# Keys, queries and the turn of the maxima computed by halves of the rows, each half at its own part of a stretch over two PSUM banks

## The reference

```python
h = _ln(x, g1, be1)
x = _attn(h, h, Wq1, Wk1, Wv1, Wo1, bo1) + x        # 16 heads of 64, 1024 keys for each of 1024 queries
h = _ln(x, g2, be2)
x = _attn(h, context, Wq2, Wk2, Wv2, Wo2, bo2) + x  # 64 keys
h = _ln(x, g3, be3)
y = h @ Wp + bp
a, gate = (y[..., :FF_HID], y[..., FF_HID:])
x = a * jax.nn.gelu(gate, approximate=False) @ W2 + b2 + x
```

## Time and profile before

| | us |
|---|---|
| median of 3 runs | 2045.64 (2045.41 to 2047.96) |
| the profiled execution | 2048.6 |
| its span | 2046.8 |
| TensorE busy in it | 2031.4 (99%) |
| ScalarE, VectorE, GpSimd busy | 1156.6, 1393.2, 1416.5 |

### The profile page before, as it was taken

One profiled execution on the slowest core, in us unless ns is written; L12 is line 12 of the kernel. 1 busy time (PEld: TensorE's weight loads), 2 busy tenths in 40 slices (PEclk: granted clock), 3 DMA queues, 4 the chain that ended last, 5 costly groups with the idle time before them and its releaser, 6 DMA issues.

```text
span 2046.8 us, 31824 instructions
## 1 busy us (share of the span) xinstructions
PE 2031.4 (99%) x12500; PEld 1387.6 (68%) x12500; DVE 1393.2 (68%) x2130; ACT 1156.6 (57%) x1845; POOL 1416.5 (69%) x745
## 2 busy tenths in 40 slices
PE   8999999999999999999999999999999999999999
PEld 6655655667566566665655666566558999888888
DVE  5767678665767785568678566757777888744453
ACT  4556567554556775356667544656665667533332
POOL 2599799984988998779799867979895576300000
PEclk9999999999999999999999999999999999999999
DMA  7300000001000000010000001000011420000100
GB/s 227 124 6 21 6 6 16 6 6 45 18 11 6 16 6 6 1 62 6 6 6 22 6 1 51 7 6 1 22 42 21 145 83 1 1 21 21 42 11 31
DMA packets 46565, 58.74 MB, mean 29 GB/s; under 512 B 5968, under 2 KB 40400, under 8 KB 45264
## 3 DMA queue, kind: packets, MB, share of 16 engines
q1 hardware_dynamic: 46416, 56.71, 8.9%
HBM read 38.88 MB, written 17.83 MB: 28 GB/s over the span
## 4 chain that ended last, share of the span: by engine, by line
PE 98%; DVE 1%; ACT 1%; issue 0%; DMA 0%; DVEq 0%; ACTq 0%
PE score L490 22%; PE score L473 18%; PE score L599 9%; PE score L477 6%; PE score L421 5%; PE attn_project L613 4%; PE attn_project L585 4%; PE first_score L447 4%; PE score L555 4%; PE attn_project L421 4%; PE attn_project L524 3%; PE score L433 3%; PE score L524 2%; PE attn_project L447 2%; PE first_score L514 2%; PE attn_project L433 1%
## 5 line engine op out<-in xcount | busy, mean ns | idle before, releaser
L1317 POOL TENSOR_TENSOR acc<-acc,pT 128x1024 f32<-128x1024 f32 x384 | 914.7, 2382 | 55.9 <-POOL acc L1317 1.3
L1101 ACT ACTIVATE pT<-score 128x1024 f32<-128x1024 f32 x512 | 525.7, 1027 | 102.9 <-PE score L477 60.2
L473 PE MATMUL score<-qk 64*128 64x512 f32 x3072 | 456.3, 399 | 1.5 <-ACT oT L1112 0.9
L490 PE MATMUL score<-pT,vT 128*64 128x512 f32 x2016 | 446.5, 595 | 0.0
L780 DVE TENSOR_REDUCE nmax<-first_score 128x1 f32<-128x512 f32 x512 | 347.9, 679 | 6.9 <-PE first_score L447 4.8
L780 DVE TENSOR_REDUCE nmax<-attn_project 128x1 f32<-128x512 f32 x512 | 347.1, 678 | 0.0
L473 PEld LDWEIGHTS score<-qk 64*128 64x128 f32 x3072 | 257.2, 184 | 120.7 <-ACT pT L1101 68.2
L490 PEld LDWEIGHTS score<-pT,vT 128*64 128x64 f32 x2016 | 139.2, 137 | 289.3 <-issue 251.8
L1314 POOL TENSOR_TENSOR acc<-pT 128x1024 f32<-128x1024 f32 x64 | 154.0, 2407 | 154.5 <-ACT pT L1101 154.4
L802 DVE RECIPROCAL sums<-sums 128x512 f32<-128x512 f32 (+1 forms) x65 | 214.4, 3299 | 57.5 <-ACT sums L1126 56.9
L477 PE MATMUL score<-shift,pick 64*128 64x512 f32 x1024 | 205.3, 391 | 0.0
(11 more groups left out here) (160 smaller groups left out, 3062.1 us busy)
## 6 DMA issues: line engine op xcount, KB each, us to landing
xres<-x_middle SPq DMA_DIRECT2D x10, 512.0 KB, 3.8
xres<-in_x SPq DMA_DIRECT2D x4, 1024.0 KB, 7.6
raw_qk<-in_L_xattn_Wq SPq DMA_DIRECT2D x32, 128.0 KB, 2.2
raw_qk<-in_L_xattn_Wk SPq DMA_DIRECT2D x32, 128.0 KB, 2.4
raw_v<-in_L_xattn_Wv SPq DMA_DIRECT2D x8, 512.0 KB, 4.0
keys_all<-keys SPq DMA_DIRECT2D x1, 4096.0 KB, 12.0
values_all<-values SPq DMA_DIRECT2D x1, 4096.0 KB, 12.4
out_x<-xres SPq DMA_DIRECT2D x7, 512.0 KB, 2.9
```

The source lines that it names most:

```text
L473: e.matmul(bank, qk[P % 2][r, 2 + h, keys], qk[P % 2][r, w, queries], start=(part == 0), stop=False)
L490: last = e.matmul(banks[bank][head * DH:(head + 1) * DH, :], vT[:, v_slot(D, jt), c0:c0 + DH], pT[:, jt, head, :], start=(jt == 0), stop=( ...
L1101: e.activation(pT[:, jt].rearrange("p h n -> p (h n)"), SC[R % 2][:, :], ACT.Exp).then_inc(s.exponential, 1)
L1317: e.tensor_tensor(total, total, pT[:, jt], ALU.add).then_inc(s.probs_added, 1)
```

## The change

In the 43 plain spells the work is done by halves of the rows. The maxima's transpose becomes two, each of 64 rows, one to the last 64 columns of T0 and one to the first 64 of T1, which together are one stretch of 128 columns over two banks. A projection becomes four runs of six matmuls of 64 rows by 256 columns: rows 0 to 63 and rows 64 to 127 of the operands are multiplied side by side, each half into its own half of a stretch of 512 columns, whose first 256 are the end of one bank and whose last 256 are the start of the next; then (`turn` 1) they change over, and each half adds to what the other has written. In between stands the same run of the other projection, and a new semaphore, `half_projected`, keeps the change-over behind the end of both halves' first turn. The first projection now goes to the stretch over PV and PJ, the second to the one over S1a and S1b. ScalarE and VectorE read the stretches in one instruction as before, in the same order. In the rounds that follow a plain spell, the part 1 of `first_score` is moved from round 1 to round 0. Nothing is changed in the other spells.

```diff
+        HALF = BANK // 2
+        across = {"S1": SC[1][:, HALF:HALF + BANK], "PX": PX[:, HALF:HALF + BANK],
+                  "T": FS[:, BANK - DH:BANK + DH]}
+        both = {"S1": ("S1a", "S1b"), "PX": ("PV", "PJ"), "T": ("T0", "T1")}
...
-            jobs = [("max", C + 1, "T1")] if C + 1 < NC else []
...
+            jobs = [("max", C + 1, "T1" if between else "T")] if C + 1 < NC else []
...
-                jobs += [("qk", after, 1 - c, "S1b"), ("qk", after, 3 - c, "PJ")]
+                jobs += [("qk", after, 1 - c, "S1b" if between else "PX"), ("qk", after, 3 - c, "PJ" if between else "S1")]
...
+            def project_qk_rows(P, u, pair, turn):
...
+                if turn:
+                    need.wait_ge(s.half_projected, half_of[P, u])
+                else:
+                    bank_free(*both[pair])
+                for i, (w, h) in enumerate(TERMS):
+                    for k in range(KT):
+                        for g in range(2):
+                            r, part = slice(g * DH, (g + 1) * DH), (g + turn) % 2 * HALF
+                            last = e.matmul(across[pair][:, part:part + HALF], wqk[r, P % 2, w, kind, k, :],
+                                            hT[r, h, k, c * BANK + part:c * BANK + part + HALF],
+                                            start=(i == k == turn == 0), stop=(i == 2 and k == KT - 1 and turn == 1))
+                            if i == 2 and k == KT - 1 and not turn:
+                                last.then_inc(s.half_projected, 1)
+                if turn:
+                    last.then_inc(s.qk_projected, 1)
+                    for bank in both[pair]:
+                        free[bank] = ((s.split_lo, qk_of[P, u]),)
...
+            def turn_max_rows(C):
...
+                bank_free(*both["T"])
+                for g in range(2):
+                    r = slice(g * DH, (g + 1) * DH)
+                    last = e.transpose(across["T"][:, r], maxima[r, :], ident[r, r])
+                last.then_inc(s.max_turned, 1)
+                for bank in both["T"]:
+                    free[bank] = ((s.shift_in, C + 1),)
...
-                    if job[0] == "qk":
+                    if job[0] == "qk" and job[-1] in both:
+                        project_qk_rows(*job[1:], 0)
...
+                for job in jobs:
+                    if job[0] == "qk" and job[-1] in both:
+                        project_qk_rows(*job[1:], 1)
...
-                        for head in range(2):
-                            first_score(*next_part(C + 1, jt), head)
+
+                        early = C > 0 and by_rows(C - 1)
+                        for part in {0: (0, 1), 1: ()}.get(jt, (jt,)) if early else (jt,):
+                            for head in range(2):
+                                first_score(*next_part(C + 1, part), head)
```

More of the change, by code:

```diff
@@ L21 @@
     const mask_made padded wqk_split wv_split ffn_split probs_added bias_added bias3_added scaled2 keys2_lo
-    ctx_turned ctx_product wq2_turned keys2_product values2_product ln_turned qk_projected v_projected first_scored0 first_scored1
+    ctx_turned ctx_product wq2_turned keys2_product values2_product ln_turned qk_projected half_projected v_projected first_scored0 first_scored1
     max_turned scored attended summed out1_product scored2 turned2 out2_product up_product down_product
@@ L308, in slot, with by_rows @@
             if after < B * PAIRS:
-                jobs += [("qk", after, 1 - c, "S1b"), ("qk", after, 3 - c, "PJ")]
+                jobs += [("qk", after, 1 - c, "S1b" if between else "PX"), ("qk", after, 3 - c, "PJ" if between else "S1")]
             return jobs
+        def by_rows(C):
+            return slot(C) and slot(C)[0][-1] == "T"
+        half_of = {job[1:3]: 2 * (i + 1) for i, job in enumerate(
+            job for C in range(NC) for job in slot(C) if job[0] == "qk" and job[-1] in both)}
         def last_out1(i):
@@ L412, in fold_values @@
                     free[bank] = ((semaphore, n + 1),)
+            def project_qk_rows(P, u, pair, turn):
+                kind, c = (1 if u < 2 else 0), u % 2
+                need.wait_ge(s.wqk_split, 2 * (P + 1))
+                normed((1, P // PAIRS * CHUNKS + c))
+                if turn:
[15 more added lines that the diff above has]
+                        free[bank] = ((s.split_lo, qk_of[P, u]),)
             def project_qk(P, u, bank="PJ"):
@@ L458, in turn_max @@
                 free[bank] = ((s.shift_in, C + 1),)
+            def turn_max_rows(C):
+                need.wait_ge(s.max_in, C + 1)
+                need.wait_ge(s.const, 2)
+                bank_free(*both["T"])
[5 more added lines that the diff above has]
+                    free[bank] = ((s.shift_in, C + 1),)
             def score(R, part, head):
@@ L530, in whole_array @@
                 for job in jobs:
-                    if job[0] == "qk":
+                    if job[0] == "qk" and job[-1] in both:
+                        project_qk_rows(*job[1:], 0)
+                    elif job[0] == "qk":
                         project_qk(*job[1:])
@@ L534, in whole_array @@
                         project_v(*job[1:])
+                    elif job[0] == "max" and job[-1] in both:
+                        turn_max_rows(job[1])
                     elif job[0] == "max":
@@ L773, in split_qk @@
                 hi, lo = (qk[P % 2][:, 2 * kind + w, span] for w in range(2))
-                e.scalar_tensor_tensor(lo, banks[bank], SCALE if kind == 0 else 1.0, hi.bitcast(F32),
+                e.scalar_tensor_tensor(lo, across[bank] if bank in both else banks[bank], SCALE if kind == 0 else 1.0,
+                                       hi.bitcast(F32),
                                        ALU.mult, ALU.subtract).then_inc(s.split_lo, 1)
@@ L795, in make_shift @@
                 e.tensor_tensor(shift[:, :].rearrange("p (t n) -> p t n", t=TPC),
-                                banks[bank][:, 0:PART].unsqueeze(1).to_broadcast([PART, TPC, PART]),
+                                (across[bank] if bank in both else banks[bank])[:, 0:PART].unsqueeze(1).to_broadcast(
+                                    [PART, TPC, PART]),
                                 mask[:, :].unsqueeze(2).to_broadcast([PART, TPC, PART]), ALU.mult).then_inc(s.shift_in, 1)
@@ L1081, in split_qk @@
                     need.wait_ge(s.scored, 4 * TILES * (P - 1))
-                e.activation(qk[P % 2][:, 2 * kind, c * BANK:(c + 1) * BANK], banks[bank], ACT.Copy,
+                e.activation(qk[P % 2][:, 2 * kind, c * BANK:(c + 1) * BANK],
+                             across[bank] if bank in both else banks[bank], ACT.Copy,
                              scale=SCALE if kind == 0 else 1.0).then_inc(s.split_hi, 1)
```

## The result

The changed kernel takes 2063.75 us, median of 4 runs (2062.69 to 2064.64), the kernel before 2046.80 in the same comparison (2045.41 to 2048.59): a ratio of 1.0079, 95% interval 1.0066 to 1.0091, **slower by 0.8%**. The forecast was 2063.0. The profiled execution took 2064.18 against 2048.6, +15.6 us, where the sum had said +17.4; the medians are 16.95 apart.

The account below looks back on a forecast made before the run. TensorE, busy 99% of the span, was taken to bound the kernel. 41 spells at +0.42 us (17.2) and +0.23 once gave +17.4: 2063.0 us beside the median of 2045.64, own range 2059 to 2070 (chance 0.70).

Parts of the forecast that it names:

- the sum: Whole execution: 41 plain spells at +0.42 us, 17.2, and +0.23 once, together +17.4 us.
- The passage, -0.20: From projections into round 0: array stays divided and weights load ahead, saving 0.20 us per plain spell.
- The projections, +0.09: Per plain spell, 24 pairs of 256 columns at 0.120 take 2.88 us instead of 2.79: +0.09.
- The halved transpose: Maxima's turn: two side-by-side transposes for one, first projection starts as before; bounds 0.05 us either way.
- the lower bound: Projection pairs at 0.116 us, half of 0.233: the low end of the forecast's own range, -3.9 us.
- The change-over at no cost: Between projection turns: the wait for half_projected costs nothing, as the other projection's six pairs, 0.72 us, stand between.
- The wait at round 1: Round 1's first pair waits for VectorE's lo part of the second projection to free S1: new wait of 0.29 us.
- The ring: Rounds: bank reuse takes 2.34 to 2.36 us, TensorE's matmuls 2.33; no slack, so round 3 stays as late as round 1.
- the rival that the last rounds would make it good: Only TensorE's own time counts: -0.11 us per spell, -4.5 in all, 2041.1 us; chance 0.10.
- The moved pair, +0.23 in the list for round 1: The first_score pair moved to round 0 stands ahead of round 1: +0.23 us there, which round 2 gets back.
- Pairs at 0.108: Rival: projection pairs take 0.108 us, 0.29 off each spell, 2051.1 us; chance 0.08.
- an instruction floor: Rival: TensorE takes four records no faster than 0.216 us, projections 5.18 us per spell, 2157 us; chance 0.07.

Follow-up runs that it names:

- e4_max_only: The changed kernel with whole-array projections again and no pair moved, so only the maxima's turn is by halves: 2054.85 us, ratio 1.0034.
- e5_turns_together: The kernel of e3_no_late_bank with both turns of a projection one after the other: 2070.93 us, ratio 1.0114 to the kernel before.
- e1_whole_s1_last: The kernel before with two banks exchanged: in plain spells the first projection goes to PJ, the second to S1b. 2060.26 us, ratio 1.0060.
- e7_stretches_swapped: The changed kernel with the first projection over S1, the second over PV and PJ, and no pair moved: 2071.63 us, ratio 1.0114.
- e2_pair_back: The changed kernel with the moved pair of first_score put back into round 1: 2064.78 us, ratio 1.0077 to the kernel before.
- e3_no_late_bank: The changed kernel with projections over S1a/S1b, then T1/PJ, maxima's halves in T0 and PV, no pair moved: 2042.28 us, ratio 0.9970.

## Why the prediction was right

- *The passage, -0.20.* Right: in the changed kernel the projections run into round 0 without a gap, and e4_max_only, which adds a passage, pays 0.15 net of a shorter transpose.
- *The projections, +0.09.* The step was right and the term too large. I took 0.120 per pair from the feed-forward rows; the pairs take 0.118, 24 of them 2.83, +0.04. These 0.05 are about the difference between 0.42 forecast and 0.38 measured per spell, or 17.4 and 15.6 us. The halved transpose, put at nothing, gave nothing: the first pair works from 643.06 - 2.83 = 640.23, 0.18 behind the turn, before 0.16. Half of the 512-column spacing, which I had kept as the lower bound, was the nearer row.
- *The change-over at no cost.* Right; e5_turns_together shows its price, 0.35 twice per spell, when its cover is gone.
- *The wait at round 1.* Right in place, releaser and size: a load that starts 0.05 behind VectorE's lo part, 42 times (one of which was there before), and 0.29 lost, as forecast. The trace has round 1 at 0.39 behind where it was, the forecast 0.41.
- *The ring.* Right. Round 3 is as late as round 1, and rounds 4 to 7 give nothing back. Against the rival that the last rounds would make it good stand e1_whole_s1_last and e7_stretches_swapped: both keep the delay to the end. But they do not show the ring, since a TensorE that works in program order without idle time would keep it too. The ring is seen where TensorE got time back and lost it again, behind the spell C = 61, where no bank is late and only the moved pair is different. Rounds 1, 2, 3 and `attend`, before (turn at 1482.88) and in the changed kernel:

```profile
1485.59 0.40 PE L477 MATMUL score<-shift,pick 64*128 64x512 f32 x2
...
1486.77 0.40 PE L477 MATMUL score<-shift,pick 64*128 64x512 f32 x2
...
1487.93 0.40 PE L477 MATMUL score<-shift,pick 64*128 64x512 f32 x2
...
1494.16 2.37 PE L490 MATMUL score<-pT,vT 128*64 128x512 f32 x10
```

```profile
1498.26 0.27 PE L505 MATMUL first_score<-ident,maxima 64*128 64x64 f32 x2
...
1501.21 0.40 PE L527 MATMUL score<-shift,pick 64*128 64x512 f32 x2
...
1502.15 0.40 PE L527 MATMUL score<-shift,pick 64*128 64x512 f32 x2
...
1503.57 0.40 PE L527 MATMUL score<-shift,pick 64*128 64x512 f32 x2
...
1509.79 2.79 PE L540 MATMUL score<-pT,vT 128*64 128x512 f32 x12
```

```profile
1502.75 0.53 PEld L523 LDWEIGHTS score<-qk 64*128 64x128 f32 x6 [0.41 <-ACT pT L1164]
```

  From the turn, round 1 is 0.24 late (2.95 for 2.71), round 2 not at all (3.89 both), round 3, whose load waits for the exponential of round 1, 0.26 again (5.31 for 5.05), and `attend` 0.25 (11.53 for 11.28). That is the +0.23 once of the sum; in e2_pair_back the time to `attend` is 11.29.
- *The moved pair, +0.23 in the list for round 1.* As an item of the list it was right, but the list misled: since the start of round 1 is set by the bank, e2_pair_back without the move is no better. In a plain spell the move and the wait are one term of 0.52, not two of 0.23 and 0.29. Only behind the spell C = 61, where no bank is late, does the move cost by itself.
- *Pairs at 0.108, and an instruction floor.* Both out: 0.118 in the changed kernel. Two loads and two matmuls came every 0.118 us over 48 matmuls in a row, so four records in 0.216 was no floor. The Trainium skill (TensorE: Matmul & The Clock Gate, Back-to-back issue gap) has 262 cycles for 256 columns, 0.109 us at 2.4 GHz, and no run here reaches this with these operands. The 62 ns per matmul that the Trainium skill has for one way of decoding (same page, "Wait — 56ns, not 53.3ns?") would be 0.124 for a pair, an estimate, and the pairs come faster than that.
- *What was not computed.* That the same halves could be had without the wait: the forecast named the bank and the time at which it was wanted, and the step from there to e3_no_late_bank (the second projection into the two banks wanted last, T1 and PJ) was a matter of placing.

## What to carry to other kernels

A gain on the engine that bounds the kernel counts only if the next thing that it needs is free by then. Before moving a result to other banks, write down for each bank when it is let go and when it is next wanted. The result that is finished last belongs in the banks that are wanted last. Where two buffers go round between two engines and a round of the one takes as long as a round of the other (here 2.33 and 2.34 us for two), a delay is not made good, so 0.3 us at one place is 0.3 us in every period. And compare stretches inside the traces before whole spans, which here differ by up to 4 us (first turn at 64.2 to 68.3 us) from what lies ahead of the change.

## What the runs showed that I had not expected

The two halves of the array can run apart. In e1_whole_s1_last only head 1's bank is late, and head 0's matmuls of round 1 went ahead as far as program order let them: the round's six L473 stretch over 1.17 us instead of 0.85, with head 0 one matmul ahead, and they come side by side again in round 3, whose loads wait for the exponential of round 1. Of round 1's fourth products head 0's came 0.10 late and head 1's 0.33, and the exponential, which needs both, started at 643.64, 0.43 behind head 1's instead of the usual 0.47; so round 3 lost 0.29 of the 0.32 that I had worked out. What made these last 0.04 is not shown. And split operands of 256 columns stand at 0.117 to 0.118 us here, whole or divided, against 0.120 in the feed-forward part of the same kernel; what makes that difference stays open.
